# Four chained attention layers on one core: a rewritten order of TensorE's steps, alternating head pairs in layer 0, merged maximum-row DMAs, 14 probability buffers, five dummy matmuls

## The reference

```python
# layer 0: 4 heads of 4 channels, softmax over the query axis
A = softmax(q^T k, axis=-2);  y = gamma * (Wo (v A) + bo);  x = x + y
# layer 1: one head, q and k of 16 channels, v of 128
x = x + gamma * (v softmax(q k)^T)
# layer 2: 8 heads of 16 channels; q from group_norm(x),
#          k and v from group_norm of the 2x2 average-pooled x (256 positions)
x = x + wproj (softmax(q k^T / 4) v)
# layer 3: one head of 128 channels on group_norm(x) with 32 groups
x = x + out_w (softmax(q k^T / sqrt(128)) v) + out_b
```

## Time and profile before

| | us |
|---|---|
| median of three runs | 434.34 |
| the profiled execution | 433.25 |
| its span, first to last instruction | 431.2 |
| PE / DVE / ACT / POOL busy within the span | 375.4 / 252.0 / 187.2 / 53.3 |
| mean granted clock of TensorE | 0.865 of full speed |

### The profile page before, as it was taken

The page is one execution under the profiler, slowest core; times in us unless marked ns, Lnnn a source line. Parts: engine busy times, 40 slices in busy tenths (PEclk is TensorE's granted clock), DMA queues, the critical chain, the costliest instruction groups (busy, mean ns, idle before and its releaser), DMA issues.

```text
span 431.2 us, 4565 instructions
## 1 busy us (share of the span) xinstructions
PE 375.4 (87%) x1756; PEld 162.1 (38%) x1756; DVE 252.0 (58%) x312; ACT 187.2 (43%) x228; POOL 53.3 (12%) x36
## 2 busy tenths in 40 slices
PE   5689789999899989877998898987988997899994
PEld 2245222334223342333442342453444233364541
DVE  1876776775845575383666345695296016592733
ACT  3034478856533357902365534215404571513210
POOL 4000000000006400000000043200420000300820
PEclk9685699988869985976599998988995899999998
DMA  7000000000000000000000000000000000000011
GB/s 277 0 0 2 0 1 3 0 2 0 2 1 2 0 0 0 3 0 3 0 1 2 2 0 0 0 0 2 1 3 1 2 2 0 0 2 0 2 49 49
DMA packets 1508, 4.44 MB, mean 10 GB/s; under 512 B 352, under 2 KB 720, under 8 KB 1360
## 3 DMA queue, kind: packets, MB, share of 16 engines
q1 hardware_dynamic: 1488, 4.16, 2.6%
HBM read 2.99 MB, written 1.05 MB: 9 GB/s over the span
## 4 chain that ended last, share of the span: by engine, by line
PE 65%; DVE 19%; ACT 5%; issue 5%; DMA 3%; SPq 2%; ACTq 0%; DVEq 0%
PE attn_acc L869 12%; PE attn_acc L863 9%; DVE neg_max L604 7%; PE products L834 6%; PE products L756 5%; PE products L838 5%; PE products L760 4%; PE products L823 3%; PE products L828 3%; PE products L768 3%; PE products L784 3%; DVE neg_max L601 3%; ACT probs L495 3%; PE products L898 2%; DVE neg_max L607 2%
## 5 line engine op out<-in xcount | busy, mean ns | idle before, releaser
L495 ACT ACTIVATE probs<-products 128x1024 f32<-128x1024 f32 x128 | 127.1, 1023 | 111.5 <-PE products L828 32.0
L604 DVE TENSOR_REDUCE neg_max<-products 128x2 f32<-128x1024 f32 x64 | 76.2, 1220 | 32.6 <-PE products L784 28.3
L869 PE MATMUL attn_acc<-probs,v 128*128 128x512 f32 x128 | 64.0, 612 | 0.0
L863 PE MATMUL attn_acc<-probs,v 128*32 128x512 f32 x384 | 59.6, 713 | 0.0
L601 DVE TENSOR_REDUCE neg_max<-products 128x4 f32<-128x1024 f32 x32 | 37.4, 1217 | 19.4 <-PE products L797 19.3
L366 POOL TENSOR_TENSOR prob_sum<-prob_sum,probs 128x1024 f32<-128x1024 f32 x16 | 38.5, 2405 | 72.7 <-ACT probs L495 71.6
L366 POOL TENSOR_TENSOR prob_sum<-probs 128x1024 f32<-128x1024 f32 x4 | 9.4, 2356 | 286.2 <-ACT probs L495 262.0
L607 DVE TENSOR_REDUCE neg_max<-products 128x1 f32<-128x1024 f32 x32 | 37.4, 1218 | 11.7 <-PE products L789 4.9
L784 PE MATMUL products<-rounded_b,rounded_a 32*128 32x512 f32 x128 | 35.3, 567 | 9.4 <-DVE neg_max L604 5.7
L823 PE MATMUL products<-rounded_a,rounded_b 32*128 32x512 f32 x128 | 34.6, 566 | 7.4 <-DVE neg_max L604 1.9
L838 PE MATMUL products<-rows_a,rows_b 128*128 128x512 f32 x64 | 31.9, 623 | 0.0
(11 more groups left out here) (124 smaller groups left out, 390.1 us busy)
## 6 DMA issues: line engine op xcount, KB each, us to landing
w<-w_rest SPq DMA_DIRECT2D x1, 1235.0 KB, 7.9
x<-x SPq DMA_DIRECT2D x2, 512.0 KB, 4.4
y<-x SPq DMA_DIRECT2D x2, 512.0 KB, 2.6
tmp<-row_selector SPq DMA_DIRECT2D x1, 512.0 KB, 8.7
rounded_a<-max_rows SPq DMA_DIRECT2D x16, 2.0 KB
w<-w_first SPq DMA_DIRECT2D x1, 146.0 KB, 2.2
rows_a<-max_rows SPq DMA_DIRECT2D x8, 2.0 KB
rows_a<-max_rows SPq DMA_DIRECT2D x8, 4.0 KB
```

The lines of the kernel that those rows point to most:

```text
L495: nc.scalar.activation(P[:, n % NP, :], slot(s), ACT.Exp, scale=SCALE[L]).then_inc(read_act, 1)
L604: nc.vector.tensor_reduce(out=m[:, 2 * t:2 * t + 2], in_=slot(s).rearrange("p (a n) -> p a n", a=2), op=ALU.max, axis=AX.X, negate=True).t ...
L863: mm = nc.tensor.matmul(acc[32 * j:32 * j + 32, h], lhs, P[:, b_no[q] % NP, halves[a]], start=t0 == 0 if L == 0 else t0 % 2 == 0, stop=t0 ...
L869: mm = nc.tensor.matmul(acc[:, h], V13[b][:, t0, :], P[:, b_no[q] % NP, h], start=t0 == first, stop=t0 == last)
```

## The change

1. `ORDER` is a new string with the same letters in the same numbers (129 P, 128 A, 128 B, 26 N, 24 E, 16 T, 9 V, 2 Y). It begins k, q, k, one A, q, v, so that both images' layer-0 projections come ahead of or among the first A steps. The first P is the 45th step instead of the 30th.
2. Layer 0's group g now has head pair g % 2 and column half g // 2.
3. The two (layer 0) and four (layer 2) DMAs of maximum rows become one each, with a destination that steps over 32 partitions.
4. `NP` is 14 instead of 8.
5. DVE clears a 128 x 256 tile at its start, and PE multiplies it five times (fp32, into the first PSUM tile) ahead of its first real step. A step kind `W` is also added, for dummy matmuls inside the order, but the string has no W.

The diff; the accumulators' and selectors' indices follow the new numbering and are shown once:

```diff
--- before.py
+++ after.py
...
 RING = 3
-MAX_DMAS = {0: 2, 1: 4, 2: 4, 3: 1}
-NP = 8
+MAX_DMAS = {0: 1, 1: 4, 2: 1, 3: 1}
+NP = 14
+WARMUP = 5
 POOL_SUM = 6
...
 ORDER = (
-    "NNAAAAAAANNAVATAAABABABAABVBAPTAABPAABBABAABPBABPT"
-    "ABAPABAPBABPBABABAPTBPPABBPABBPBBAPBBAPAPABPBABBPT"
-    "AAVPPPBAEAEBABEBABPNNVABABBPTAAAPPPABABABABABBPTBA"
-    "BAPAPABPPBABPAPPBAPPAPBABPPAPBAPATPBPPAPABPAAPEPBB"
-    "BEBBTNPBBNPPBPNBPBNNBBBBPBVPPAAPAAPAAAAEATEABEBBBA"
-    "AANNAVABABBPTABAAPBABABAPBAPPABBPBBETPPPPEBEBYEPBE"
-    "PPPNBNPPBPNNBPPAAPABPAPPBAPPAAEPAPEVNTNBNPNNBBPBAA"
-    "PAVAAPAAPAPPATAAPPABABABABABPTBBBPBBBPBPPBBBPPBEPP"
-    "PEEYEENBNBBNNBAAPAAPPAPAAAPVPTPPBBBPBEPBPBEPPPPPBP"
-    "PBPPPPPPEPPE"
+    "NNNANVAAVAAAAAAATAABAABAABABAATBBABABAABBAABPABPAT"
+    "BPBBAPAPBPABBPVAABPPBTAPBPABBBABABABAPBAAPATPBABPA"
+    "PBBPBPBAAPPEBEBPAEBPAANNBAAVAABPTAAABABBATPABPBPBA"
+    "BPBBBAPAPPBBAPAABAPAPABAPTPBBAPPPAPBBBPPPPBBAPPBEA"
+    "PEPTBBNBBBPNBPBNNPBPAPBAPAPBABPAPAPAEANETAVEBBABAA"
+    "NABNAVABABATPBAPABBAPBAAPPBABBAPETBBBEPPPPBEBYEPBE"
+    "NPPBBNPPPPNNPBBAPPAAPAPAPBAPPAEPAPETVNBNBPNNNABAAP"
+    "AAPVPAPAABAATAPAAPBAPPBABBABPTBBBPBBBPPPBBBPBBEPPP"
+    "EEPBEYENBNPBNNPPAAPAAPABAPAAVPTPEBBPPBEPPPPPBBPBPP"
+    "BBPPPPPPEPEP"
 )
...
     following = {c: iter(s) for c, s in steps.items()}
+    following["W"] = (("warm", i) for i in range(len(ORDER)))
     return [next(following[c]) for c in ORDER]
...
     for s in plan:
-        if s[0] == "out" and (s[1] in (1, 3) and s[3] or s[1] == 0 and s[3] % 2):
-            o_tile[s[1:]] = o_tile[(*s[1:3], s[3] - 1)]
+        if s[0] == "out" and (s[1] in (1, 3) and s[3] or s[1] == 0 and s[3] > 1):
+            o_tile[s[1:]] = o_tile[(*s[1:3], s[3] - (2 if s[1] == 0 else 1))]
         elif s[0] == "out":
...
+        zeros = sb("zeros", [128, NKV])
+
         ps = ctx.enter_context(nc.psum_tensor("products", [128, RING, N], F32))
...
         cleared = sem("cleared")
+        zeroed = sem("zeroed")
         consts_ready, consts_act = sem("consts_ready"), sem("consts_act")
...
                     if L == 0:
-                        for a in range(2):
-                            row = GROUP * (2 * (g // 2) + a) + ONE
-                            sp.dma_start(RA[b][row:row + 1, halves[g % 2]].bitcast(F32),
-                                         ZR[4 * a:4 * a + 4, i, :]).then_inc(maxrows_in[b], 16)
+                        row = GROUP * 2 * (g % 2) + ONE
+                        sp.dma_start(RA[b][row:row + GROUP + 1:GROUP, halves[g // 2]].bitcast(F32),
+                                     ZR[0:8, i, :]).then_inc(maxrows_in[b], 16)
                     elif L == 1:
...
                     elif L == 2:
-                        for j in range(4):
-                            row = GROUP * j + ONE
-                            sp.dma_start((FA, FB)[g][b][row:row + 1, :], ZR[8 * j:8 * j + 8, i, :]).then_inc(maxrows_in[b], 16)
+                        sp.dma_start((FA, FB)[g][b][ONE:ONE + 3 * GROUP + 1:GROUP, :],
+                                     ZR[0:32, i, :]).then_inc(maxrows_in[b], 16)
                     else:
...
                         wait_read(act, last)
-                    h = halves[s[3] % 2] if L == 0 else slice(0, N)
-                    nc.scalar.activation(O[o_tile[u]][:, h], acc[:, h], ACT.Identity).then_inc(acc_out, 1)
+                    h, bank = (halves[s[3] // 2], halves[s[3] % 2]) if L == 0 else (slice(0, N), slice(0, N))
+                    nc.scalar.activation(O[o_tile[u]][:, h], acc[:, bank], ACT.Identity).then_inc(acc_out, 1)
                 elif kind == "y" and L == 0:
...
+            nc.vector.memset(zeros[:, :], 0.0).then_inc(zeroed, 1)
             nc.vector.memset(eps[:, 0:1], EPS)
...
+            pe.wait_ge(zeroed, 1)
+            for i in range(WARMUP):
+                nc.tensor.matmul(slot(jobs[0])[:, 0:NKV], zeros[:, 0:128], zeros[:, :], start=True, stop=True)
             for s in plan:
                 kind, L, b = s[0], s[1], s[2] if len(s) > 2 else None
+                if kind == "warm":
+                    following = next(p for p in plan[plan.index(s):] if p in job)
+                    if job[following] >= RING:
+                        wait_read(pe, jobs[job[following] - RING])
+                    nc.tensor.matmul(slot(following)[:, 0:NKV], zeros[:, 0:128], zeros[:, :], start=True, stop=True)
+                    continue
                 if kind == "ya":
...
                     if L == 0:
-                        mh, (mt, nh) = g % 2, divmod(t, 2)
+                        mh, (mt, nh) = g // 2, divmod(t, 2)
                         for a in range(2):
-                            rows = slice(GROUP * (2 * (g // 2) + a), GROUP * (2 * (g // 2) + a) + GROUP)
+                            rows = slice(GROUP * (2 * (g % 2) + a), GROUP * (2 * (g % 2) + a) + GROUP)
                             tile = slice(HALF * mh + 128 * mt, HALF * mh + 128 * (mt + 1))
...
                         for a in range(2):
-                            rows = slice(GROUP * (2 * (g // 2) + a), GROUP * (2 * (g // 2) + a) + GROUP)
+                            rows = slice(GROUP * (2 * (g % 2) + a), GROUP * (2 * (g % 2) + a) + GROUP)
                             mm = nc.tensor.matmul(slot(s)[:, halves[a]], RB[b][rows, 128 * t:128 * (t + 1)],
-                                                  RA[b][rows, halves[g % 2]], start=True, stop=True)
+                                                  RA[b][rows, halves[g // 2]], start=True, stop=True)
                     elif L == 1:
...
                                 j = 2 * i + a
-                                lhs = V0[b][:, 2 * (g // 2) + a, 2 * t0 + i, :] if L == 0 else V2[b][:, g, t0 % 2, j, :]
+                                lhs = V0[b][:, 2 * (g % 2) + a, 2 * t0 + i, :] if L == 0 else V2[b][:, g, t0 % 2, j, :]
                                 mm = nc.tensor.matmul(acc[32 * j:32 * j + 32, h], lhs, P[:, b_no[q] % NP, halves[a]],
...
                         pe.wait_ge(den_acc, den_no[("PV1", L, b, g, 7, 0)])
-                    parts = {0: [(O[o_tile[(0, b, 2 * p)]], w("pick0")[:, 36 * p:36 * p + 36]) for p in range(2)] if L == 0 else [],
+                    parts = {0: [(O[o_tile[(0, b, p)]], w("pick0")[:, 36 * p:36 * p + 36]) for p in range(2)] if L == 0 else [],
                              1: [(DS, w("ones4"))], 2: [(O[o_tile[(L, b, g)]], w("sel2"))], 3: [(DS, w("ones4"))]}[L]
...
                             mm = nc.tensor.matmul(slot(s)[64 * p:64 * p + 64, h], w("w0o")[:, 64 * p:64 * p + 64],
-                                                  O[o_tile[(0, b, 2 * p)]][:, h], start=True, stop=True)
+                                                  O[o_tile[(0, b, p)]][:, h], start=True, stop=True)
                     full(s, mm)
```

## The result

The changed kernel took 402.26 us (median of 4 runs) against 434.13 us, a ratio of 0.9222 with a 95% interval of 0.9132 to 0.9311. Measured once more later, six runs gave 401.55 us and 0.9241 (0.9192 to 0.9289). The ratios leave out runs that took over 1.5% longer than the fastest of their kernel and the medians don't, so the two differ where runs spread widely. The change is 32 us faster; the prediction had the direction and 18 us of it.

What follows compares the result with a forecast made beforehand. TensorE was taken as the bound, busy 375.4 of 431.2 us, with up to 49 us lost to half clock. Gains of 24.6 us less 6.2 took 433.25 to 414.9, plus 1.1 to the median: 416 us, range 401 to 430.

Steps and rivals of the forecast that it cites:

- the set-off: One new half-clock stretch, given no place, sized like that from 31.3 to 44.9 us: 6.2 us set against the gains.
- half of 10.2 us: Layer 2, image 0: 10.2 us clock price plus 3.1 us idle time, half of the 13.3 us taken: 6.6 us gain.
- half of 6.1 us: Stretch from 324.8 to 338.5 us: clock price 6.1 us at half clock, perhaps half of it won: 3 us gain.
- the 5.5 us of layer 0: New order in layer 0, image 0, keeps DVE fed: half of the remaining 10.8 us taken as gain.
- the stretches left as they are: Other half-clock stretches, among them four from 92.7 to 171.2 us: no gain forecast.
- the fourth transpose: Sign in layer 0, image 0: the fourth unit's maxima are transposed at 58 to 62 us instead of 67.
- The dummies: Five warm-up matmuls at the start let k and q run partly at high clock: 1.5 us gain, bounds -0.7 and +3.
- The merged DMAs: One maximum-row DMA instead of four shortens waits before layer 2's first B steps: 5 us gain; layer 0 nothing more.
- Head pairs: Alternating head pairs in layer 0: 0 us gain, bounds half a microsecond each way.
- The group norm: Layer 2, image 1: layer 3's first B step goes ahead of the norm, filling PE's 3.21 us wait: 3 us gain.
- All of it comes: Rival: DVE kept fed in layer 0, all named waits and clock losses go, 39.9 us to 394.5 us; chance 0.2.
- Slower by the clock: Rival: layer 0 of both images at half clock throughout, 16 us more less 6.5 us gains, 444 us; chance 0.1.

Runs made afterwards that it cites:

- experiment 2: Kernel before with only the new order string and 14 buffers: 408.39 us, ratio 0.9417 to the kernel before.
- experiment 12: experiment 1 with 37 dummy matmuls added at the two places where the new order gained most: 435.74 us, ratio 0.9935 to the kernel before.
- experiment 1: Changed kernel with the old order string put back, all else kept: 426.31 us, ratio 0.9711 to the kernel before.
- experiment 4: Changed kernel with the maximum-row DMAs split as before, two a unit in layer 0 and four in layer 2: 408.33 us, ratio 0.9372.
- experiment 8: Changed kernel with seven GpSimd sums of probabilities moved to DVE: 395.90 us, ratio 0.9044 to the kernel before.
- experiment 7: Changed kernel with layer 0's old numbering, head pair g // 2 and half g % 2: 400.11 us, ratio 0.9212 to the kernel before.

## Why the prediction was right and where it was wrong

**The step that failed is the set-off together with the halves before it**: the clock's share in the sum. The prediction gave the order 18.1 us less 6.2 us for one new half-clock stretch, 12 us; experiment 2 shows 25. The terms for the clock that it named were half of 10.2 us, half of 6.1 us and the set-off of -6.2, which is some 2 us net, beside what the 5.5 us of layer 0 has of it. By the profiles the clock gave back 25.4 us and idle time 10.3. The stand-still was sized well: PE idle for about 45 us was forecast and 45.5 measured.

The set-off's new stretch didn't come: layer 0 of image 0 is at the low clock for 30.7 us as before (10.2 + 13.6 + 6.8 us then), and in the rest of the kernel the half-clock time fell from some 82 to 27 us. Row by row of the table, the 17 us missing from the forecast are the set-off's 6.2, 4.0 in each of the two stages with halves, 2.4 in the stretches left as they are, and small ones.

The reason is in what experiments 2 and 12 show together. A stretch that lacks work for PE pays twice, by the gap and by the work done at half clock in and after it. Useful steps from a neighbouring unit removed both (idle 3.8 to 2.7 us and clock 0.82 to 1.00, idle 5.8 to 2.0 us and clock 0.65 to 0.99 in the windows above); dummies removed only the clock's part, at their own price. The prediction valued each stretch at half for fear that the clock would not hold, and where useful work was there it held in full. That the order is the cause of these 21 to 25 us is shown, by taking it out and by running it alone; which moves within the new string did it is argued from the windows and not tested one by one.

**The stretches left as they are.** From 158 to 184 us the prediction gave nothing. The first A step of layer 2 of image 0 started at 168.1 instead of 184.0 us, partly since it stands nine steps earlier in the order; from the broadcast of layer 1 to y of that layer 13.7 us were gained against 9.7 forecast.

**Layer 0** was right for the fourth transpose, 60.4 us for a forecast of 58 to 62, but the reason was half wrong. 2.9 of the 6.6 us are the dummies' early start, which three of the six profiles with them lost in part or whole, and 3.7 the order (67.0 to 63.3 in experiment 2). DVE wasn't kept fed: its bound of 54.8 us stayed 5.6 us away.

**The dummies** were sized at 1.5 us and are worth nothing that can be measured; that the start at 1.2 us and the end by 5.5 us were about right (1.19 and 4.9 to 5.6) didn't help.

**The merged DMAs**: 5 us forecast, 6 measured, of which 3.4 are visible waits, 0.9 of them in layer 0, which the prediction put at nothing. That one DMA with all rows costs no more than one of the four was right, 0.55 against some 0.66 us.

**Head pairs and buffers** were right at nothing beyond what the order needs.

**The group norm**: the wait before image 1's norm fell from 3.21 to 1.23 us, 2 of the 3 us. But the prediction didn't see that GpSimd can stop DVE. The row was in the trace of the kernel before, where one such operation took 2.26 us; in the changed one it happened three times, and two waits for q grew from 1.8 and 1.4 to 4.2 and 2.7 us. That is the real set-off, 3.7 us.

**The rivals.** "All of it comes", with a chance of 0.2, was nearest by its time: some 30 us for 404. The clock losses of layers 2 and 3 did go as it says, but layer 0 was not fed as it says. "Slower by the clock" named the right danger. Its mechanism came true where the old order ran with the other parts: in experiment 1's profile, the slowest of its six executions, layer 0 was at the low clock for 54.6 us and the fourth transpose came at 71.8 us, 4.8 later than before; the profile of experiment 12 has the same 54.6 and 71.7. It didn't decide, since the gains of later stages don't hang on layer 0.

## What to carry to other kernels

Where TensorE's work is fed by another engine, sum the half-clock windows with the busy time in them before anything else; half of that busy time is the most that the clock can give back to a denser order of useful steps, and here that was 25 of the 36 us by which the profiled span fell. Of three tries at filling gaps with dummy work one didn't raise the clock at all and two paid for it what it was worth or more, and the warm-up ahead of a stage that DVE feeds didn't last: the clock fell again at 17.7 us. Look for tiny DVE operations that take a GpSimd operation's length: moving seven sums won more than the warm-up, the head pairs and three of the buffers together.

## What the runs showed of the hardware that was not expected

PE busy for 60.2 of 61.4 us stayed at the low clock for the whole time (one filler ahead of each A step), while with two fillers it was at the high clock, with 16.0 of 16.0 us busy. PE's busy share in the profile alone doesn't tell which clock is granted. The Trainium skill (TensorE: Matmul & The Clock Gate, Part 1) ties the full clock to how busy PE has been; the first of these runs disagrees, if busy is what the profile counts.

The low-clock time in layer 0 varies between executions: 30.7, 44.4 and 47.8 us in the profiles of the changed kernel and of experiments 4 and 8, which share the order of layer 0. The fourth transpose came at 60.4, 66.9 and 68.8 us in them, so up to 2% of the total hang on it. One sign goes with it: of the eight profiles with dummies and no fillers in layer 0, in the three in which the dummies took 3.82, 3.98 and 4.20 us together the long low stretch lasted 30.7 us, and in the five in which they took 4.54 to 4.64 us (experiments 1, 4, 7, 8 and 12) it lasted 34.1 to 54.6. What decides it no run here shows.
